# Audio tower, one core: the attention's query, key and value products as three products of rounded halves in place of fp32 products

## What is computed

```
h = _L0_tok_ref(x, L0_tok_w)                              # softmax pooling of two steps
h = h + _L0_attn_ref(_layernorm(h), ...)                  # RWKV: k, v, r products, a scan
h = h + _L0_ffn_ref(_layernorm(h), ...)                   # 192 -> 768 -> 192, gelu
h = h + _L1_attn_ref(_layernorm(h), ...)                  # attention, 12 heads of 16
h = h + _L1_ffn_ref(_layernorm(h), ...)                   # 8 experts, the top 2 of each token

def _L1_attn_ref(x, Wq, Wk, bk, Wv, bv, gq, gk, Wo, bo):
    q = layernorm_nobias(x @ Wq.T, gq)
    k = layernorm_nobias(x @ Wk.T + bk, gk)
    v = x @ Wv.T + bv
    scores = jnp.einsum('bnqd,bnkd->bnqk', q, k) * scale
    attn = jax.nn.softmax(scores, axis=-2)
    o = jnp.einsum('bnqk,bnkd->bnqd', attn, v)
    return o @ Wo.T + bo + x
```

## Time and profile before

| | |
|---|---|
| median of the runs | 1742.29 us (three runs, 1734.06 to 1750.06) |
| the profiled execution | 1717.65 us, of which span 1715.9 us |
| mean granted TensorE clock in it | 0.926 |
| PE busy | 1559.2 us (91%), 10985 matmuls |
| DVE busy | 1372.5 us (80%) |
| ACT busy | 1185.0 us (69%) |
| POOL busy | 724.6 us (42%) |
| DMA | 139.71 MB, 81 GB/s |

### The profile page before, as it was taken

How to read it: one execution, slowest core, us unless ns; L and a number is a source line. 1 busy time by engine, 2 the same in 40 slices (tenths; PEclk the granted TensorE clock), 3 DMA queues, 4 the chain that set the end, 5 groups by cost and what they waited for, 6 DMA issues and landing times.

```text
span 1715.9 us, 33844 instructions
## 1 busy us (share of the span) xinstructions
PE 1559.2 (91%) x10985; PEld 1263.6 (74%) x10985; DVE 1372.5 (80%) x2826; ACT 1185.0 (69%) x3268; POOL 724.6 (42%) x742
## 2 busy tenths in 40 slices
PE   4488999999999999999999998789899999999986
PEld 3366777777677677677677676668799999999976
DVE  6788788788678788788688753458899989999996
ACT  2357887887787887888788777576566666666552
POOL 1121133233232332333232222234677767777775
PEclk8799998998989999998899888669999999999988
DMA  4000011011011011011010000155776766676662
GB/s 125 28 29 29 13 61 41 23 60 39 25 53 37 34 53 37 34 53 40 31 53 22 32 27 17 57 163 150 196 170 164 170 161 169 160 172 168 150 164 50
DMA packets 116557, 139.71 MB, mean 81 GB/s; under 512 B 20881, under 2 KB 95362, under 8 KB 116482
## 3 DMA queue, kind: packets, MB, share of 16 engines
q1 hardware_dynamic: 87120, 107.30, 20.5%
q0 software_dynamic: 26592, 29.92, 9.3%
q10 hardware_dynamic: 2770, 1.56, 0.3%
HBM read 91.36 MB, written 42.44 MB: 78 GB/s over the span
## 4 chain that ended last, share of the span: by engine, by line
PE 65%; DVE 14%; ACT 13%; issue 5%; SPq 2%; DMA 1%; POOL 0%; DVEq 0%; POOLq 0%; ACTq 0%
PE ps L955 12%; PE ps L970 8%; PE ps L790 7%; ACT probs L1213 5%; PE ps L867 4%; PE ps L972 4%; PE ps L776 4%; PE ps L825 3%; PE ps L668 3%; PE ps L813 2%; PE ps L883 2%; PE ps L782 2%; PE ps L627 2%; DVE nmax L1745 2%; PE ps L674 2%
## 5 line engine op out<-in xcount | busy, mean ns | idle before, releaser
L1485 POOL DMA_INDIRECT out<-ey,etoken x142 | 250.1, 1761 | 136.6 <-DMA out<-ey,etoken 65.8
L1213 ACT ACTIVATE probs<-ps,nmax 128x128 f32<-128x128 f32 x768 | 270.7, 401 | 25.1 <-DVE nmax L1745 24.9
L1259 ACT ACTIVATE h_full<-ps,eb 128x512 f32<-128x512 f32 (+1 forms) x234 | 157.9, 675 | 151.2 <-PE ps L955 151.0
L970 PE MATMUL ps<-w_hl,h_hi 128*128 128x384 f32 x852 | 252.4, 367 | 5.7 <-DVE ey L1928 5.4
L972 PE MATMUL ps<-w_hl,h_lo 128*128 128x192 f32 x852 | 215.3, 253 | 0.0
L1745 DVE TENSOR_REDUCE nmax<-ps 128x6 f32<-128x768 f32 x128 | 120.4, 952 | 108.1 <-PE ps L867 107.9
L1213 ACT ACTIVATION_READ_ACCUMULATOR probs<-ps,nmax 128x1 f32 x768 | 186.0, 242 | 0.0
L970 PEld LDWEIGHTS ps<-w_hl,h_hi 128*128 128x128 f32 x852 | 162.6, 191 | 6.2 <-issue 5.8
L972 PEld LDWEIGHTS ps<-w_hl,h_lo 128*128 128x128 f32 x852 | 165.4, 194 | 0.0
L1475 POOL TENSOR_TENSOR w_lo<-w_raw,w_hi 128x1536 fp32r<-128x1536 f32 x38 | 152.5, 4013 | 30.6 <-ACT w_hi L1239 30.5
L1889 DVE TENSOR_TENSOR h_lo<-h_full,h_hi 128x512 fp32r<-128x512 f32 (+1 forms) x234 | 154.0, 718 | 8.5 <-ACT h_hi L1260 8.0
(11 more groups left out here) (319 smaller groups left out, 3770.1 us busy)
## 6 DMA issues: line engine op xcount, KB each, us to landing
w_raw<-in_L_ffn_w SPq DMA_DIRECT2D x38, 576.0 KB, 4.8
ex<-expert_rows_in SPq DMA_DIRECT2D x32, 528.0 KB, 5.4
w_raw<-in_L_ffn_w SPq DMA_DIRECT2D x38, 384.0 KB, 5.3
w_raw<-in_L_ffn_w SPq DMA_DIRECT2D x76, 192.0 KB, 5.6
xt<-in_x SPq DMA_DIRECT2D x16, 768.0 KB, 4.5
hA_kept<-hA SPq DMA_DIRECT2D x16, 384.0 KB, 2.6
out<-resC SPq DMA_DIRECT2D x16, 384.0 KB, 2.6
expert_rows_in<-xt SPq DMA_DIRECT2D x9, 528.0 KB, 6.0
```

Source lines behind the costliest of these rows:

```text
L970: nc.tensor.matmul(ps[:, 4 + s, 0:2 * C], h_hi[b][:, m, q], w2_hl[b][:, m, :], start=(m == 0), stop=False)
L1213: last = nc.scalar.activation(probs[:, t % 2, HJ * c + j, :], ps[:, 4 + j, c * P:(c + 1) * P], ACT.Exp, bias=nmax[:, t, j, c:c + 1], accum ...
L1259: nc.scalar.activation(h_full[:, m, 0:n], ps[:, m % 4, 0:n], ACT.Gelu, bias=eb1[u][:, m:m + 1])
L1485: nc.gpsimd.indirect_dma_start(total, bass.IndirectOffsetOnAxis(ap=etoken[u][:, s:s + 1], axis=0), ey[b][:, s, :], None, bounds_check=NB * ...
```

## The change

`hTC` becomes of type fp32r (rounded by the copy that writes it), and `hTC_lo` holds what the rounding left out: a new VectorE step `c_low` subtracts `hTC` from the PSUM bank. The weights are split once in the same way by `qkv_halves`, in `fill` of round 1; their fp32 copy now lies in a tile, `probs`, that is not yet in use then. Each fp32 product becomes three fp32r products: high by high, low by high, high by low. The last product (low by low) is left out. In the second block of `c_qkv` the terms are the outer loop and n the inner. TensorE now waits for `c_low` where it waited for `hTC`. The router's input goes to a tile of its own, `hTR`. `c_low` stands behind `a_mix` in `fill` and between `c_attn_add(1)` and `c_attn_add(2)` in `round_`.

```diff
-        w_qkv = sg("w_qkv", [P, KC, 2, C + C // 2])
-        b_raw = sg("b_raw", [P, 2 * C])
+        qkv_hi = sg("qkv_hi", [P, KC, 2, C + C // 2], F32R)
+        qkv_lo = sg("qkv_lo", [P, KC, 2, C + C // 2], F32R)
...
-        hTC = sg("hTC", [P, KC, N])
+        hTC = sg("hTC", [P, KC, N], F32R)
+        hTC_lo = sg("hTC_lo", [P, KC, N], F32R)
+        hTR = sg("hTR", [P, KC, N])
...
+        w_qkv = probs[:, 1, :, :].rearrange("p h q -> p (h q)")[:, 0:KC * 3 * C].rearrange("p (k n f) -> p k n f", k=KC, n=2)
+        b_raw = probs[:, 1, :, :].rearrange("p h q -> p (h q)")[:, KC * 3 * C:KC * 3 * C + 2 * C]
...
             def c_qkv(g, ts):
-                pe.wait_ge(S["c_hT"], g + 1)
+                if isinstance(g, int) and g == 0:
+                    pe.wait_ge(S["qkv_split"], 1)
+                pe.wait_ge(S["c_low"], g + 1)
+                terms = ((hTC, qkv_hi), (hTC_lo, qkv_hi), (hTC, qkv_lo))
...
                     for n in range(2):
-                        nc.tensor.matmul(o(t, n), hTC[:, n, t * T:(t + 1) * T], w_qkv[:, n, n, :],
-                                         start=True, stop=False)
+                        for k, (x, w) in enumerate(terms):
+                            nc.tensor.matmul(o(t, n), x[:, n, t * T:(t + 1) * T], w[:, n, n, :],
+                                             start=(k == 0), stop=False)
...
                 for t in ts:
-                    for n in range(2):
-                        last = nc.tensor.matmul(o(t, n), hTC[rest(n), 1 - n, t * T:(t + 1) * T],
-                                                w_qkv[rest(n), 1 - n, n, :], start=False, stop=True)
+                    for k, (x, w) in enumerate(terms):
+                        for n in range(2):
+                            last = nc.tensor.matmul(o(t, n), x[rest(n), 1 - n, t * T:(t + 1) * T],
+                                                    w[rest(n), 1 - n, n, :], start=False, stop=(k == 2))
                     last.then_inc(S["qkv_psum"], 1)
...
-                        last = nc.tensor.matmul(ps[:, 6, t * E:(t + 1) * E], hTC[rows, k, t * T:(t + 1) * T],
+                        last = nc.tensor.matmul(ps[:, 6, t * E:(t + 1) * E], hTR[rows, k, t * T:(t + 1) * T],
...
-                if gr is not None: transposed(gr, "r", hTC, 4)
+                if gr is not None: transposed(gr, "r", hTR, 4)
...
+            def qkv_halves():
+                nc.vector.tensor_copy(qkv_hi[:, :, :, :], w_qkv[:, :, :, :]).then_inc(S["qkv_high"], 1)
+                dve.wait_ge(S["qkv_high"], 1)
+                nc.vector.tensor_tensor(qkv_lo[:, :, :, :], w_qkv[:, :, :, :], qkv_hi[:, :, :, :].bitcast(F32),
+                                        ALU.subtract).then_inc(S["qkv_split"], 1)
+
+            def c_low(g):
+                dve.wait_ge(S["c_hT"], g + 1)
+                nc.vector.tensor_tensor(hTC_lo[:, :, :], ps[:, 4:6, :], hTC[:, :, :].bitcast(F32),
+                                        ALU.subtract).then_inc(S["c_low"], 1)
...
                 if ga == 0: up_halves()
+                if ga == 1: qkv_halves()
+                if gc is not None: c_low(gc)
                 a_exponents(ga)
...
                 if gr is not None: c_attn_add(gr, 1)
+                if gc is not None: c_low(gc)
                 if gr is not None: c_attn_add(gr, 2)
```

More of the change, by code:

```diff
@@ L302, in build_tower @@
             oproj_psum h_kept hB_ready
-            b_stats b_rstd b_hn b_hT_psum b_hT b_low up_high up_split up_psum hid_ready down_psum hC_ready
+            b_stats b_rstd b_hn b_hT_psum b_hT b_low up_high up_split c_low qkv_high qkv_split up_psum hid_ready down_psum hC_ready
             c_stats c_rstd c_hn c_hT_psum c_hT
```

## The result

| | before | after |
|---|---|---|
| median of 20 runs each | 1735.18 us | 1744.66 us |
| the profiled execution | 1717.65 us | 1745.13 us |
| its mean granted clock | 0.926 | 0.931 |
| PE busy | 1559.2 us | 1543.5 us (x11241) |
| DVE busy | 1372.5 us | 1413.3 us |

The ratio of the two is 1.0053 with a 95% interval of 1.003 to 1.0076. The changed kernel is slower by some 9 us, or half a per cent. That is inside the forecast's "within 1%", but ten times the +0.9 us of its sum.

The account below looks back on a forecast made before the run. ScalarE's fixed list, starting when t=0 of the first half is done, was taken to bound each round and hide the second half. +2.9 - 2.0 = +0.9 us on the 1742.3 us median gave 1743 us, range 1725 to 1759.

Parts of the forecast that it names:

- within 1%: Whole kernel: forecast that the time changes by less than one per cent, 17.4 us, either way; chance 83%.
- its sum: Whole kernel: +2.9 us for twelve loop rounds and -2.0 us where the second half counts, together +0.9 us.
- The sum of a round: One loop round: +0.66 + 0.11 - 0.42 - 0.11 = +0.24 us.
- The wait for `c_low`: TensorE's start of `c_qkv` in a loop round: 516.48 in place of 515.82, +0.66 us.
- L813, now L821, with the first matmul behind the wait: First half of `c_qkv`: cheaper 128-row products -0.42 us, first matmul behind a VectorE wait +0.11 us.
- The 64-row products: First half, up to the first result: pairs run side by side, 0.63 us against 0.74, -0.11 us.
- rival 4: Loop rounds: `c_low` uncovered and 64-row products unpaired, 12 x 1.15 = 14 us, 1756 us; chance 10%.
- The cover: VectorE in a loop round: 3.43 us idle before `hTB_lo` absorbs the 0.45 us delay.
- The last groups: Groups 13 to 15: first half +0.16 us, second half 0.61 faster, -0.45 us each, -1.35 in all.
- The gain in `fill`: `fill` of round 2, where ScalarE waits for the second half: `c_low` covered, -0.61 us.
- rival 3: Clock falls at the products as TensorE waits before `c_qkv`: 13 x 1.36 = 17.7 us, 1760 us; chance 13%.
- wrong above 63: Sign against the forecast: loop rounds at full clock lasting above 63 us, where about 62.2 was expected.

Follow-up runs that it names:

- dve_only: Kernel before plus an idle VectorE subtraction of `c_low`'s size at its places, result unused, nobody waiting; 1726.23 us, ratio 0.9971 to before.
- before_again: The kernel before, unchanged, profiled once more; 1736.13 us, mean granted clock 0.934.
- wait_only: Kernel before plus `c_low` and TensorE's wait for it, products still fp32; 1744.35 us, ratio 1.0071 to before.
- hi_first: Changed kernel with t=0 and t=1 banks swapped and TensorE waiting for `hTC_lo` only ahead of t=0's last term; 1740.3 us, ratio 1.0032 to before.
- t1_first: Changed kernel, first half starting with two t=1 terms whose banks `c_low` does not read, then waiting for it; 1737.93 us, ratio 1.0044 to before.
- early_low: Changed kernel with `c_low` earlier on VectorE, first half ahead of `c_project(2)`, `c_attn_add(2)` behind `a_scan_p`; 1735.86 us, ratio 1.0023 to before.

## Why the prediction was right, and where it was not

**The sum of a round: right, and to 0.01 us by luck.** Forecast +0.24 us, measured +0.25. The mechanism holds: ScalarE's list hides the second half, and the wait eats the gain of the first. But the terms are off by -0.09, +0.15, -0.06 and +0.01, which cancel:
- The wait for `c_low`: forecast +0.66, measured +0.57; `c_low` takes 1.21 us (forecast 1.23), TensorE starts 0.05 behind it (0.04), and it begins 2.47 us behind the `vpad` of t=3, where the forecast's 515.21 is 2.55 behind.
- L813, now L821, with the first matmul behind the wait: forecast -0.42 + 0.11 = -0.31. A block is 782.40 - 781.51 = 0.89 us where it was 0.97, twice: -0.16. The step was right (0.127 forecast, 0.13 measured); missing was the first matmul of a block behind the bf16 bias, 0.23 instead of 0.13, so the second t does not save what the step says. The bias matmuls, which the forecast left as they were, give back 0.06.
- The 64-row products: forecast -0.11, measured 784.36 - 783.65 = 0.71 against 0.81, -0.10. They run in pairs side by side (0.13 us from one pair to the next), so that part of rival 4 fell.
- In true fp32 a product took 0.485 us, and three fp32r matmuls take 0.39. The Trainium skill, "FP8 and Floating Point Precision", section "TensorE Precision Notes", has fp32 as four passes, which for three gives an estimate of 0.364 us. The trace has 0.39, so the measurement decides: an fp32r matmul of 288 columns costs more than a quarter of an fp32 product. With the first matmul of the block a product comes to 0.89 / 2 = 0.445 us, so that the gain is 0.04 and not 0.10.

**The cover: right.** `hTB_lo` kept its 3.48 us, and dve_only shows 0.0. The other part of rival 4 fell too.

**The last groups: half right.** In the one shown below the second half's copy comes 1043.31 - 1036.67 = 6.64 us behind the first product, where before it was 7.46; less the later start that is -0.25 a group, forecast -0.45. The gain in `fill` is within what two executions of one kernel differ by (the first product of group 0 comes at 125.04 us, in before at 123.61, in before_again at 125.99), and can't be told.

```profile
1036.67 0.40 PE L821 MATMUL ps<-qkv_hi,hTC 128*128 128x288 f32 x1 [0.53 <-DVE hTC_lo L1752]
...
1043.31 0.49 ACT L1210 ACTIVATE qk<-ps 128x384 f32<-128x384 f32 x1 [0.74 <-PE ps L828]
```

**The step that failed: the clock.** The sum took the time at the low clock as the same before and after. In five of seven comparisons, each with before on the same chip, it is not: 0.006 to 0.011 less of mean clock with the three terms, some 9 us. For the first 20 runs themselves this is inferred from the later series, and that the change causes it is not shown: no run says how it would. It is rival 3 in its sign and at half its price, but not in its mechanism: at the products the granted clock is 1.00 in every round of the loop, in all fourteen traces, before's among them. The time at the low level lies 15 to 25 us and 40 to 60 us behind the first product, where before had it too; in four traces with three terms it reaches on up to the next first product. Single executions scatter too much to place the rest: the loop has 34 to 96 us at the low level in the four traces with fp32 products, and 65 to 106 in the nine with three terms. The prediction weighed where the clock might fall by what stands beside the change; there it did not fall. The Trainium skill, page "TensorE: Matmul & The Clock Gate", section "HAM oscillation — how this bites in real kernels", describes such falls for a product whose tiles wait for a DMA longer than their matmuls last. TensorE's idle time before `c_qkv` is 0.41 us, and wait_only, which has the whole wait, has 0.9329 against 0.9331: twelve runs show no lower clock from the wait by itself, at a standard error of 0.003.

**A second step that failed: the reading of the profiled execution.** The prediction put its 24.6 us under the median down to less time at the low clock. Its clock of 0.926 is below the mean of before's runs on each chip on record (0.9295 to 0.9375), so it had more. It was fast because it lacks the late releases: its middle lasts 47.6 us against 48.5 and more in twelve rounds, 11 us or more, and its part behind group 12 is 16 us shorter than in before_again. "Rounds differ by the clock alone" holds inside that trace, and not from one execution to the next. So the signs worked out from it, 62.2 us a round and wrong above 63, were too low: before_again itself, without the change, has 62.86 to 62.89. The forecast's 1743 us against 1744.66 is near by luck: the three runs it started from have their median 7 us above that of all 20, of which they are the first three. From 1735.18 the same sum would give 1736, some 9 us short.

## What to carry to other kernels

A wait that a new step brings is dear where the consumer's start sets the round: here 1.2 us of VectorE cost nothing as work and 0.57 to 0.71 us a round as a wait (S3 of the changed kernel against before and against hi_first). Order the terms of a split product so that those without the new half come first, into banks that the splitting engine doesn't read; that turned +0.25 us a round into -0.44 without any other change. But add a saving on TensorE to the total only with the granted clock of many runs beside it, and compare it with the old kernel's on the same chip: hi_first wins 5 us on the path and yet is no faster than before, at a mean clock lower by 0.011.

## What the runs showed of the hardware

- VectorE was released late by TensorE's products: 3.67 to 3.80 us from the start of L896 or L905 to `c_attn_add(0)`, against 2.05 where no such delay is. It was there in all eleven traces from three chips and not in the one from a fourth; the medians of the unchanged kernel on them, 1731 to 1735 and 1719.6 us, go with it. What delays it isn't settled.
- The first fp32r matmul behind bf16 matmuls took 0.23 us, the next 0.13, at 288 columns; behind a wait the first took 0.24, and right behind fp32 matmuls 0.26 (hi_first, 782.22 to 782.48).
- The mean granted clock was lower by 0.006 to 0.011 in five of seven comparisons of kernels with three fp32r terms in place of fp32 products, while it stayed at 1.00 at the products themselves; in the other two, t1_first and early_low, by 0.003 and 0.001. The unchanged kernel's own mean went from 0.9295 to 0.9375 between four chips.
